# Reordering the opening of a two-block kernel in halves, and adding the last residual in HBM by accumulating DMAs

## The reference

```python
x = x + layernorm(mamba_block(layernorm(x)))      # block 1: norm, projection, conv, scan, gate, projection
x = x + layernorm(fp8_linear(layernorm(x)))       # block 2: one 128x128 linear layer, fake fp8
```

```python
x_in, z = split(x @ W_in + b_in)
xc      = silu(causal_conv(x_in, conv_w) + conv_b)
B, C    = split(xc @ W_xp + b_xp)
delta   = softplus(xc @ W_dt + b_dt)
h[t]    = exp(delta[t] * A) * h[t-1] + (delta[t] * xc[t]) * B[t]     # A = -exp(A_log), 16 states per channel
y       = (h . C + D_skip * xc) * silu(z)
out     = layernorm(residual + y @ W_out + b_out, alpha, beta)
```

## Time and profile before

| what | value |
|---|---|
| median of 3 runs | 639.04 us (636.86 to 639.94) |
| the profiled execution | 639.14 us, its span 637.4 us |
| busy, PE / DVE / ACT / POOL | 85% / 79% / 69% / 47% of the span |
| first `drive_unit` starts, first scan starts | 41.44 us, 43.64 us |
| first `scale_x` of the tail starts | 595.45 us |
| last store is issued | 634.43 us |

### The profile page before, as it was taken

One profiled execution on the slowest core, in us unless ns is written; L12 is line 12 of the kernel. 1 busy time (PEld: TensorE's weight loads), 2 busy tenths in 40 slices (PEclk: granted clock), 3 DMA queues, 4 the chain that ended last, 5 costly groups with the idle time before them and its releaser, 6 DMA issues. The chain is left out here.

```text
span 637.4 us, 10358 instructions
## 1 busy us (share of the span) xinstructions
PE 542.6 (85%) x2893; PEld 419.1 (66%) x2893; DVE 504.8 (79%) x1001; ACT 441.9 (69%) x885; POOL 300.7 (47%) x333
## 2 busy tenths in 40 slices
PE   4979899999899988998999899998999797861571
PEld 3557687787678866876687767786778686660120
DVE  4036698979887988799979878888989989974695
ACT  2466985799659874989498938894799586702364
POOL 2042343656455563458255826373647465401374
PEclk9979999999899999999999999999999999977555
DMA  7000535053502460155115420624052506510012
GB/s 209 22 1 1 100 67 100 1 100 66 101 2 55 79 134 1 33 99 107 25 33 99 87 47 9 123 46 86 1 112 54 99 10 124 106 27 0 1 51 82
DMA packets 19184, 39.84 MB, mean 62 GB/s; under 512 B 3648, under 2 KB 9920, under 8 KB 19136
## 3 DMA queue, kind: packets, MB, share of 16 engines
q0 software_dynamic: 9216, 33.56, 26.7%
q1 hardware_dynamic: 9920, 5.78, 3.3%
HBM read 3.68 MB, written 2.10 MB: 9 GB/s over the span
## 5 line engine op out<-in xcount | busy, mean ns | idle before, releaser
L1200 DVE TENSOR_TENSOR_SCAN state<-decay,drive 128x512 f32<-128x512 f32 x256 | 297.2, 1203 | 30.7 <-PE drive L995 24.9
L995 PE MATMUL drive<-diag,uT 128*128 128x256 f32 x1024 | 245.9, 384 | 0.7 <-ACT uT L731 0.7
L745 ACT ACTIVATE decay<-delta,a_neg 128x510 f32<-128x510 f32 x256 | 170.5, 730 | 54.8 <-DVE state L1200 53.9
L995 PEld LDWEIGHTS drive<-diag,uT 128*128 128x128 f32 x1024 | 187.1, 193 | 21.7 <-ACT uT L731 1.0
L1011 PE MATMUL hT<-ident,state 128*128 128x128 f32 x1024 | 143.0, 278 | 24.3 <-DVE acc_d L1223 19.1
L1011 PEld LDWEIGHTS hT<-ident,state 128*128 128x128 f32 x1024 | 119.8, 143 | 56.3 <-issue 26.1
L500 POOL TENSOR_SCALAR_AFFINE_SELECT diag<-Bt 128x512 f32<-128x512 f32 x128 | 92.1, 725 | 74.5 <-PE drive L995 58.2
L766 ACT ACTIVATE term<-hT,Ct 128x256 f32<-128x256 f32 x256 | 102.9, 484 | 8.8 <-PE hT L1011 8.8
L516 POOL DMA_DIRECT2D acc<-term x64 | 59.9, 935 | 24.1 <-DMA acc<-term 11.8
L1223 DVE SCALAR_TENSOR_TENSOR acc_d<-hT,Ct,acc_d 128x256 f32<-128x256 f32 x160 | 66.5, 470 | 4.4 <-PE hT L1011 4.3
L938 PE MATMUL fbank<-xnT,w_tap 128*128 128x512 f32 x112 | 50.4, 592 | 0.0
(11 more groups left out here) (170 smaller groups left out, 624.9 us busy)
## 6 DMA issues: line engine op xcount, KB each, us to landing
acc<-term POOLq DMA_DIRECT2D x64, 512.0 KB, 4.5
out_dram<-state SPq DMA_DIRECT2D x8, 256.0 KB, 2.2
x_all<-in_L_attn_x_dram SPq DMA_DIRECT2D x2, 256.0 KB, 4.2
state<-in_L_attn_conv_w_dram SPq DMA_DIRECT2D x1, 512.0 KB, 5.4
w_in<-in_L_attn_W_in_dram SPq DMA_DIRECT2D x1, 256.0 KB, 3.2
w_dt<-in_L_attn_W_dt_dram SPq DMA_DIRECT2D x1, 256.0 KB, 5.1
w_out<-in_L_attn_W_out_dram SPq DMA_DIRECT2D x1, 128.0 KB, 3.8
w_ffn<-in_L_ffn_weight_dram SPq DMA_DIRECT2D x1, 64.0 KB, 2.4
```

The lines of the kernel that those rows point to most:

```text
L745: last = nc.scalar.activation(decay[:, g % DECAYS, h, :, s, 1:], delta[:, par, h, :, 1:], ACT.Exp, scale=a_neg[:, h, SG * g + s:SG * g + s ...
L995: last = nc.tensor.matmul(dst[:, :, P * c:P * c + P], uT[:, par, TC * b + c, P * h:P * h + P], diag[:, n % DIAGS, c, :, :], start=True, st ...
L1200: nc.vector.tensor_tensor_scan(state[:, n % STATES, h, :, :].rearrange("p s t -> p (s t)"), decay[:, g % DECAYS, h, b, :, :].rearrange("p ...
```

## The change

In the head:

- SP issues `cw_r` right after `w_in`, on a semaphore of its own, and `bin_c` behind `cw`.
- DVE makes the tap products before the rounding of the fp8 weight, takes the statistics of pair 1 next, and its shift after the rounding. PE waits for the tap products earlier in its list and for `edge_ready` only before L941 of pair 0.
- ACT applies Silu to each x_in half straight out of PSUM, without the copy; `front_norm(1)` stands before them and `front_xnT(1)` behind the first decays.
- PE's dt products run with the half of `xc` as the outer loop.
- dt's second bias is added by DVE. Min, Exp, Ln, max and the product with `xc` run in two halves with a semaphore each; DVE, not POOL, makes `u`. The transposes run half by half, and DVE copies the second `uT` bank.
- The numbers of warming transposes change (4 before the tap products, none behind them, 16 instead of 20 before the transposes of `u`).

In the tail:

- SP stores x after block 1 to the output as soon as each pair's `b_sum` is done, in the slots, 8 stores of 256 KB.
- POOL runs `round_up(g+1)` first and then issues an accumulating DMA that adds `fn` onto the output in HBM; `last_sum`, `fo` and the final stores by SP are gone. `fn` has four buffers.

```diff
-            sp.dma_start(bin_c[:, :], column(b_in), **slow).then_inc(w_in_loaded, 16)
+            sp.dma_start(cw_r[:, :, :], ...).then_inc(tap_loaded, 16)
             sp.dma_start(cw[:, :, :], ...).then_inc(conv_loaded, 16)
+            sp.dma_start(bin_c[:, :], column(b_in), **slow).then_inc(conv_loaded, 16)
             sp.dma_start(cb[:, :], column(conv_b), **slow).then_inc(conv_loaded, 16)
-            sp.dma_start(cw_r[:, :, :], ...).then_inc(conv_loaded, 16)
...
-                    sp.wait_ge(f_out, nth(grp, 1, 1))
-                    sp.dma_start(out_v[...], chunks(fo[:, par, :])).then_inc(stored[par], 16)
+                    sp.wait_ge(b_sum, nth(pr, 1, 1))
+                    sp.dma_start(out_v[...], x_k[:, bass.ds(pr.v * CH, CH), :]).then_inc(x1_stored, 16)
...
-            def last_sum(grp, par):
+            def add_to_out(grp, par):
                 pool.wait_ge(f_norm, nth(grp, 1, 1))
-                if grp.after(2):
-                    pool.wait_ge(stored[par], (grp.v - par) * 8)
-                nc.gpsimd.tensor_tensor(fo[:, par, :], fn[:, par, :], x_all[...], ALU.add).then_inc(f_out, 1)
+                pool.dma_start(out_v[...], chunks(fn[:, grp.v % 4, :]), accum_op=ALU.add)\
+                    .then_inc(stored[grp.v % 4], 16)
             def tail(grp, par):
-                if old:
-                    last_sum(*old)
                 if new:
                     round_up(*new)
+                if old:
+                    if old[0].v == 0:
+                        pool.wait_ge(x1_stored, 16 * PAIRS)
+                    add_to_out(*old)
...
+            front_norm(Pair(1), 1)
             act.wait_ge(edge_ready, TAPS + 1)
             for h in range(HALVES):
-                front_xin(Pair(0), h)
+                act.wait_ge(front_full, 1 + h)
+                nc.scalar.activation(xc[:, 0, h, :], front_bank(Pair(0), h), ACT.Silu, bias=in_bias[:, h:h + 1])\
+                    .then_inc(xin_ready, 1)
             for h in range(HALVES):
                 front_silu_z(Pair(0), 0, h)
-            front_silu_x(Pair(0), 0)
...
-            for m in range(HALVES):
-                front_dt(Pair(0), m)
-            front_norm(Pair(1), 1)
-            front_exp(Pair(0))
-            front_log(Pair(0))
+            for h in range(HALVES):
+                act.wait_ge((half_low, dt_low)[h], 1)
+                nc.scalar.activation(dt_e[:, h, :], dt_e[:, h, :], ACT.Exp).then_inc((half_exp, sp_exp)[h], 1)
+            for h in range(HALVES):
+                act.wait_ge((half_exp, sp_exp)[h], 1)
+                nc.scalar.activation(dt_e[:, h, :], dt_e[:, h, :], ACT.Ln, bias=1.0).then_inc((half_log, sp_log)[h], 1)
+            act.wait_ge(a_neg_ready, 1)
+            exp_decay(Pair(0), 0, 0)
+            front_uT(Pair(0), 0, 0)
+            for m in range(1, max(HALVES, DECAY_LEAD)):
+                exp_decay(Pair(0), 0, m)
             front_xnT(Pair(1), early=True)
...
+            for h in range(HALVES):
+                pe.wait_ge(xin_ready, 1 + h)
+                for m in range(HALVES):
+                    last = nc.tensor.matmul(front_bank(Pair(0), 4 + m), w_dt[:, h, P * m:P * m + P], xc[:, 0, h, :],
+                                            start=(h == 0), stop=(h == HALVES - 1))
...
+            for h in range(HALVES):
+                dve.wait_ge((half_log, sp_log)[h], 1)
+                nc.vector.tensor_tensor(d[:, h, :], dt_v[:, h, :], dt_e[:, h, :], ALU.max)\
+                    .then_inc((half_delta, delta_ready)[h], 1)
+                dve.wait_ge((half_delta, delta_ready)[h], 1)
+                nc.vector.tensor_tensor(u[:, h, :], d[:, h, :], xc[:, 0, h, :], ALU.mult).then_inc((half_u, u_ready)[h], 1)
+            dve.wait_ge(front_full, 9)
+            nc.vector.tensor_copy(uT[:, 0, 2:4, :], front_bank(Pair(0), 8)...).then_inc(uT_ready, 1)
```

More of the change, by code:

```diff
@@ L270, in build_sandwich @@
         conv_loaded = sem("conv_loaded")
+        tap_loaded = sem("tap_loaded")
+        half_low = sem("half_low")
+        half_exp = sem("half_exp")
+        half_log = sem("half_log")
+        half_delta = sem("half_delta")
+        half_u = sem("half_u")
         wm_loaded = sem("wm_loaded")
@@ L354, in build_sandwich @@
         f_norm = sem("f_norm")
-        f_out = sem("f_out")
-        stored = [sem("stored_even"), sem("stored_odd")]
+        x1_stored = sem("x1_stored")
+        stored = [sem("added_%d" % k) for k in range(4)]
         x_v = x.rearrange("b l d -> (b l) d").rearrange("(k p) d -> p k d", p=P)
@@ L446, in _ @@
                 for par in range(2):
-                    grp = Pair(i * 2 + par, par)
-                    sp.wait_ge(f_out, nth(grp, 1, 1))
-                    sp.dma_start(out_v[:, bass.ds(grp.v * CH, CH), :], chunks(fo[:, par, :])).then_inc(stored[par], 16)
-            for par in range(2):
-                sp.wait_ge(stored[par], 16 * PAIRS // 2)
+                    pr = Pair(i * 2 + par, par)
+                    sp.wait_ge(b_sum, nth(pr, 1, 1))
+                    sp.dma_start(out_v[:, bass.ds(pr.v * CH, CH), :], x_k[:, bass.ds(pr.v * CH, CH), :]).then_inc(x1_stored, 16)
+            sp.wait_ge(x1_stored, 16 * PAIRS)
+            for k in range(4):
+                sp.wait_ge(stored[k], 16 * PAIRS // 4)
         @block.gpsimd
@@ L868, in last_norm @@
                 act.wait_ge(f_shift, nth(grp, 1, 1))
-                if grp.after(2):
-                    act.wait_ge(f_out, grp.v - 1)
+                if grp.after(4):
+                    act.wait_ge(stored[grp.v % 4], 16 * (grp.v // 4))
                 for j in range(CH):
-                    last = nc.scalar.activation(fn[:, par, DM * j:DM * j + DM],
+                    last = nc.scalar.activation(fn[:, grp.v % 4, DM * j:DM * j + DM],
                                                 f_bank(grp.v)[:, DM * j:DM * j + DM],
@@ L939, in front_in @@
                                          xnT[:, :, tap:tap + L], start=(tap == 0), stop=False)
+                    if k == 0 and is_first(pr):
+                        pe.wait_ge(edge_ready, TAPS + 1)
                     taken = front_bank(pr, k).rearrange("p (b t) -> p b t", b=PAIR)
@@ L1381, in _ @@
             nc.vector.tensor_reduce(wq_top[:, :], fbank[0:1, 0:P], AX_X, ALU.max).then_inc(wq_max, 1)
+            dve.wait_ge(w_in_loaded, 16)
+            dve.wait_ge(tap_loaded, 16)
+            for tap in range(TAPS):
+                nc.vector.tensor_tensor(w_tap[:, tap, :], w_in[:, 0:DI], cw_r[:, :, tap], ALU.mult).then_inc(taps_ready, 1)
+            dve.wait_ge(x_second, 16)
+            front_stats(Pair(1))
             dve.wait_ge(wq_global, 1)
@@ L1393, in _ @@
             nc.vector.tensor_tensor(wqT[:, :], r, m, ALU.subtract).then_inc(wq_step, 1)
-            dve.wait_ge(w_in_loaded, 16 * 2)
-            dve.wait_ge(conv_loaded, 16 * 3)
-            for tap in range(TAPS):
-                last = nc.vector.tensor_tensor(w_tap[:, tap, :], w_in[:, 0:DI], cw_r[:, :, tap], ALU.mult)
-            last.then_inc(taps_ready, 1)
-            dve.wait_ge(x_second, 16)
-            front_stats(Pair(1))
-            dve.wait_ge(wm_loaded, 16 * 5)
-            front_low(Pair(0))
+            dve.wait_ge(xn_ready, 1)
+            front_shift(Pair(1))
+            dve.wait_ge(wm_loaded, 16 * 5)
+            dve.wait_ge(front_full, 6)
+            nc.vector.tensor_scalar(dt_v[:, 1, :], front_bank(Pair(0), 5), bdt[:, 1:2], None, ALU.add).then_inc(dt_ready, 1)
+            dve.wait_ge(dt_ready, 2)
+            for h in range(HALVES):
+                nc.vector.tensor_scalar(dt_e[:, h, :], dt_v[:, h, :], SOFTPLUS_LINEAR, None, ALU.min)\
+                    .then_inc((half_low, dt_low)[h], 1)
             dve.wait_ge(a_exp_ready, 1)
             nc.vector.tensor_scalar(a_neg[:, :, :], a_exp[:, :, :], -1.0, None, ALU.mult).then_inc(a_neg_ready, 1)
-            front_shift(Pair(1))
             front_bc(Pair(0), 0)
-            front_delta(Pair(0), 0)
+            d = delta[:, 0, :, :, :].rearrange("p h b t -> p h (b t)")
+            for h in range(HALVES):
+                dve.wait_ge((half_log, sp_log)[h], 1)
[4 more added lines that the diff above has]
+            dve.wait_ge(front_full, 9)
+            nc.vector.tensor_copy(uT[:, 0, 2:4, :], front_bank(Pair(0), 8).rearrange("p (j d) -> p j d", d=DI))\
+                .then_inc(uT_ready, 1)
             dve.wait_ge(consts_ready, 4)
```

46 lines of the change are left out of this document (23 added, 23 removed).

## The result

The kernel with the change takes 635.45 us (median of 20 runs, 632.29 to 637.79), the kernel before on the same chips 639.61 (20 runs, 635.25 to 641.71). The ratio is 0.9948, with an interval of 0.9928 to 0.9968: 0.5% faster, where 2% was forecast. The profiled execution took 635.30 us, with a span of 633.6.

The account below looks back on a forecast made before the run. No engine is full; the change touches waits between engines in the head and in the tail, where POOL and DVE block each other. Head -7.4 and tail -5.65 make -13.05 from 639.14: 626.0 us, range 620.5 to 632.5.

Parts of the forecast that it names:

- The step that failed: Slots between head and tail: the head's shift of -7.4 us reaches the end whole, so the slots change by 0.
- The end: From last norm's end to span's end: 0.1 + 4.5 landing + 0.8 close = 5.4 us, +0.9 over before.
- Rival 4: Tail: accumulating into HBM drains slowly, up to 11 us per add, end at 692; decides from 4.0 per add; chance 0.08.
- The head: Start to first drive_unit: -6.3 to dt's start, -2.55 to delta, +1.45 to drive_unit, together -7.4 us.
- as laid out: Head: DVE's four delta and u products alternate with POOL's diag_b and residual, 27.5 to 32.75; drive_unit at 34.1.
- the collision: Head, delta to drive_unit: DVE and POOL shut each other out on SBUF, making drive_unit 2.9 us late.
- Rival 1: Head without collision between DVE and POOL: -2.9 us, perhaps first unit at full clock; 621.4 to 623.2; chance 0.14.
- The tail's turns: Tail: four slow turns fall from 4.00 to 2.93 us; with unblocked shifts the last norm ends 6.55 earlier.
- Rival 2: Tail: DVE and POOL's DMA issue block each other, three turns losing 0.2 to 0.8 us; 626.6 to 628.5; chance 0.11.
- Rival 3: Tail: the add's issue grows with descriptor count; 628.4 at 2 us, 642.8 at 3.7 us; chance 0.09.
- the 1.6 that was hidden: Tail: POOL's issue of an add costs a turn nothing up to 1.6 us, before the next round_up.
- Stores in the slots at 0: Slots: the eight stores beside accumulating DMAs could cost 0 to 6 us; taken as 0.

Follow-up runs that it names:

- quiet_head: Changed kernel plus 48 DVE semaphore increments ahead of its loop, POOL holding pair 0's front_residual until u is ready; 629.01 us, ratio 0.9823 to the kernel before.
- after: The kernel with the whole change, in its first profile; 635.45 us against 639.61 before, ratio 0.9948.
- after_again: The changed kernel unaltered, run for a second profile; 635.65 us against 638.61 before, ratio 0.9956.
- stores_only: The kernel before with only the eight stores of x after block 1 added in the slots; 639.62 us against 638.61, ratio 1.0011.
- after_pad48_timed: The changed kernel with 48 semaphore increments added on DVE ahead of its loop, six runs; 628.44 us against 639.37 before, ratio 0.9845.

## Why the prediction was wrong

**The step that failed** is "After that every engine's slot goes by the others alone, so the shift should reach the end whole." It looked at waits between engines and not at where each engine's code begins, and none of the four rivals had such a loss. The new head has seven more DVE instructions, and with 147 ahead of the loop each of DVE's two jumps back costs 2.9 to 3.3 us of idle time instead of 2.0 to 2.2. Slots 2 and 4 grow by 1.4 each. Slots 3 and 5 grow by 1.9 and 2.0: 0.2 to 0.3 of each is the longer wait at the statistics (65.8 or 65.9 against 65.6 where the clock stays up), the rest a stretch at the low clock. These four make +6.7 us. With 48 instructions more all of it is gone, with 16 all but 0.5 and 0.4 in slots 2 and 4. The first stretch (+1.3) and slot 1 (-1.4) lie ahead of the first jump and cancel: 6.1 in place of 3.4 us at the low clock lie in the first stretch, and slot 1 happens to have none. Sum: 1.3 - 1.4 + 6.7 = +6.6, the whole loss.

That the number of instructions is the cause is shown, by adding seven to the kernel before and 16 or 48 to the one after. Why 147 is bad and 140, 163 and 195 are not is known only so far: the queue of instruction loads moves a third piece at the jump. What decides on the third piece isn't shown. Nor is it shown why a longer idle time of PE brings the low clock in one slot and not in another.

**The end was mis-sized**: 4.6 us more instead of 0.9. The last add is issued at 624.80 and the traffic ends at 630. Windows of the end of the changed kernel (a DMA share over 1 means packets that overlap):

```profile
620.00:624.00 4.00, 0.00 (x0) 0.00 (x0) 1.51 (x10) 3.48 (x12) 2.96 (x3) 0.50 1.31 137
624.00:628.00 4.00, 0.00 (x0) 0.00 (x0) 0.00 (x0) 0.51 (x2) 1.28 (x1) 0.50 1.34 140
628.00:630.00 2.00, 0.00 (x0) 0.00 (x0) 0.00 (x0) 0.00 (x0) 0.00 (x0) 0.50 0.76 92
630.00:632.00 2.00, 0.00 (x0) 0.00 (x0) 0.00 (x0) 0.00 (x0) 0.00 (x0) 0.50 0.00 0
```

Then nothing moves for 3 us. SP's waits show what the span ends with (L143 is the closing barrier):

```profile
SPq L458 <- DMA out_dram<-term: 43.4, 2, 41.2
SPq L143 <- PEq L143: 2.9, 1, 2.9
```

The last norm ends at 624.51. 0.3 to the issue, 5.5 to land and 3.2 to close make 9.1. The forecast had 0.1, 4.5 and 0.8. So the largest miss is the close, 2.4 us, for which the sum kept the 0.8 of a kernel that ends with a plain store: where POOL's accumulating DMA lands last it takes 3.2. What in it takes the time is open. The landing is 1.0 longer. Of this 0.4 is there with no other add ahead (4.93 for the first add); the longest landings, 6.3 and 6.1, are those of the two adds issued 0.8 and 1.9 behind another. What an add takes of the engines: q0 has (13440 - 9216) / 8 = 528 packets per add, and 30.1% of 633.6 less 26.7% of 637.4 is 20.5 us, so 2.56 us of all 16 engines per add. At 137 GB/s 256 KB take 1.9 us. Rival 4 asked this question, and its answer is 1.9 to 2.6 where 4.0 decides (its 0.33 us for a 4 KB piece belongs to the 8192 pieces of 4 KB, not to all 9216 packets, which have 0.30). With three pairs taken off the queue both terms are gone, and the piece from `scale_x` to the end is 4.7 shorter.

**The head was right**, taken over all profiles. L948 starts at 10.54 (forecast near 10.5), two of its records are slow (4.31 us), dt starts at 20.29 (20.45), `delta` 6.66 later (6.55). POOL's instructions stand between DVE's products as laid out, but the collision costs less: 6.16 from `delta` to `drive_unit` where 7.1 was forecast and 5.2 is what quiet_head reaches. The profile of the changed kernel is a lucky one. With the new head D lies between 33.08 and 35.74. The first tap product starts between 10.26 and 11.09 in all of them; most of the difference is the granted clock under the tap products. In after it is back at the full level at 11.85, and L948 to the z products takes 7.95 us; in after_again at 16.36, and it takes 10.26. The median of the ten profiles with the new head and without the wait of quiet_head is 34.7 (forecast 34.1), that of the five with the old head 41.95: 7.3 apart, where the forecast had 7.4. The first unit ran at the low clock again. Rival 1 is refuted: the collision is there (`delta` 1.75 us), and where a wait takes part of it away the end doesn't move.

**The tail's turns were right.** The `xq` are 2.91 to 2.94 apart in all turns but one (3.05), and the last norm ends 6.66 nearer to the first `scale_x` against 6.55. Rival 2 is refuted: L1500 takes 0.42 and L1531 0.14 to 0.16 with an issue beside them. The Trainium skill (SBUF — State Buffer, Who interferes with whom) lets a DVE instruction in a two-port mode hold up descriptors on GpSimd; the trace shows at most 0.05 of it, since an issue takes 1.32 to 1.33 with L1500 beside it and 1.28 without. Rival 3 holds in sign only. An issue of 528 packets takes 1.28 to 1.33 us (1.45 for the first, and one record of 1.80 that overlaps the issue before it) where one of 144 takes 0.94, and in the turns stays under the 1.6 that was hidden. By the Trainium skill (DMA: Bandwidth & Descriptors, Anatomy of one DMA) many descriptors go before the incremental cost shows. The trace bears that out only in part: the issue is far from the 3.7 of a cost in proportion, but 384 packets more do cost 0.36 us. Stores in the slots at 0 were right too, as far as stores_only can tell (ratio 1.0011, at most 1.0035).

With the jump put right the parts nearly add up: 7.5 for the head and 2.3 for the tail make 9.8, and after_pad48_timed gains 10.9. The forecast 13.05 less the 3.7 of the end is 9.4. The 1.1 that after_pad48_timed has beyond the parts fits its slots without a stretch at the low clock (D to `scale_x` 552.6 in place of 554.0).

## What to carry to other kernels

When code ahead of an engine's loop changes in length, compare the idle time at the loop's jump in both profiles before believing any other explanation of a changed loop, and try a few instructions of padding: here 48 were worth 7 us of 635. A shift made ahead of a long steady part isn't sure to reach the end; measure that part's length by itself. Work moved from an engine into a queue must be costed to the end of the program, its close included, so let the queue take the early pieces and an idle engine the last few.
